# A convolution's bias moved into the residual, its relu and sum made one DVE operation, and the order of all steps written anew

## The reference

```
# 1: convolution with gates, on the group-normalised x (pairs of channels, whole image)
info = relu(info_w @ gn(x) + info_b)            # 16 channels
mask = sigmoid(mask_w @ gn(x) + mask_b)         # 16 channels
x = x + relu(out_w @ (mask outer info) + out_b) # 256 products to 64 channels
# 2: linear attention over the 1024 pixels (tokens) of an image, 8 heads, on ln(x)
K, Q = elu(ln(x) Wk) + 1, elu(ln(x) Wq) + 1
msg = ln(attention(Q, K, ln(x) Wv) Wm)
x = x + ln(x) + ln(relu([ln(x), msg] W1) W2)
# 3: mixture of 8 experts on ln(x), the two best by a softmax gate
x = x + sum over e of weight[e] * (gelu(ln(x) W1[e] + b1[e]) W2[e] + b2[e])
```

## Time and profile before

| | |
|---|---|
| median of 3 runs | 1180.87 us |
| the profiled execution, its time | 1182.04 us |
| its span, first to last instruction | 1180.2 us |
| TensorE busy | 1080.6 us (92%) |
| DVE busy | 790.7 us (67%) |
| ACT busy | 682.4 us (58%) |
| POOL busy | 363.3 us (31%) |

### The profile page before, as it was taken

One profiled execution on the slowest core, in us unless ns is written; L12 is line 12 of the kernel. 1 busy time (PEld: TensorE's weight loads), 2 busy tenths in 40 slices (PEclk: granted clock), 3 DMA queues, 4 the chain that ended last, 5 costly groups with the idle time before them and its releaser, 6 DMA issues.

```text
span 1180.2 us, 15496 instructions
## 1 busy us (share of the span) xinstructions
PE 1080.6 (92%) x5878; PEld 487.5 (41%) x5878; DVE 790.7 (67%) x1673; ACT 682.4 (58%) x930; POOL 363.3 (31%) x277
## 2 busy tenths in 40 slices
PE   3798689989999899998999999998999989999898
PEld 1463445423544246342464335442354424634232
DVE  5675836696658876587674976669665887656534
ACT  2256365665765546765656656656566555676454
POOL 0010032243313423234312433224331343324465
PEclk9999989999999999999999999999999999999999
DMA  4010097008610195003920068100861019300580
GB/s 150 1 35 3 1 216 146 19 1 199 146 36 19 30 224 126 1 19 81 225 73 1 19 144 199 36 19 0 189 156 36 19 38 226 81 1 19 120 203 21
DMA packets 17418, 96.64 MB, mean 82 GB/s; under 512 B 3648, under 2 KB 6720, under 8 KB 13120
## 3 DMA queue, kind: packets, MB, share of 16 engines
q1 hardware_dynamic: 17344, 95.66, 34.9%
HBM read 77.82 MB, written 9.44 MB: 74 GB/s over the span
## 4 chain that ended last, share of the span: by engine, by line
PE 65%; DVE 18%; ACT 12%; issue 4%; SPq 1%; DMA 0%; DVEq 0%; POOL 0%; POOLq 0%; ACTq 0%
PE HP L809 13%; PE HP L823 10%; PE R L658 6%; PE R L614 5%; PE R L745 5%; PE R L603 4%; ACT H L957 4%; PE R L594 4%; DVE SM L1141 3%; PE R L752 2%; PE R L676 2%; PE R L667 2%; DVE TM L1290 2%; PE R L823 2%; DVE SM L1057 2%
## 5 line engine op out<-in xcount | busy, mean ns | idle before, releaser
L1002 POOL TENSOR_TENSOR XB<-TM,XB 128x512 f32<-128x512 f32 x254 | 325.2, 1298 | 663.4 <-DVE TM L1290 663.4
L957 ACT ACTIVATE H<-HP,W 128x1024 f32<-128x1024 f32 x224 | 240.5, 1113 | 129.8 <-PE HP L809 129.2
L809 PE MATMUL HP<-XF,W1E 64*128 64x512 f32 x1024 | 267.9, 631 | 20.0 <-DVE TM L1290 19.6
L823 PE MATMUL HP<-H,W 128*64 128x512 f32 x896 | 232.3, 614 | 24.4 <-ACT H L957 24.4
L1290 DVE SCALAR_TENSOR_TENSOR TM<-HP,B2S,CWB 128x512 f32<-128x512 f32 x224 | 161.3, 744 | 57.1 <-PE HP L823 56.2
L1141 DVE TENSOR_REDUCE SM<-T 128x8 f32<-128x512 f32 x128 | 84.3, 681 | 109.3 <-ACT T L892 108.1
L809 PEld LDWEIGHTS HP<-XF,W1E 64*128 64x128 f32 x1024 | 84.6, 186 | 150.0 <-DVE TM L1290 84.5
L892 ACT ACTIVATE T<-R 128x512 f32<-128x512 f32 x128 | 75.2, 604 | 83.5 <-PE R L658 77.3
L823 PEld LDWEIGHTS HP<-H,W 128*64 128x64 f32 x896 | 46.7, 135 | 172.3 <-ACT H L957 135.6
L1113 DVE SCALAR_TENSOR_TENSOR BIG<-R,T 128x512 f32<-128x512 f32 x112 | 69.6, 681 | 26.8 <-PE R L594 26.6
L614 PE MATMUL R<-W,T 128*128 128x128 f32 x512 | 73.2, 283 | 7.1 <-DVE T L1160 5.6
(11 more groups left out here) (165 smaller groups left out, 1371.0 us busy)
## 6 DMA issues: line engine op xcount, KB each, us to landing
CWB<-gates_hbm SPq DMA_DIRECT2D x32, 1536.0 KB, 21.9
CWB<-gates_hbm SPq DMA_DIRECT2D x32, 512.0 KB, 10.0
BIG<-XN SPq DMA_DIRECT2D x32, 256.0 KB, 4.5
out<-XB SPq DMA_DIRECT2D x15, 512.0 KB, 3.0
X<-x SPq DMA_DIRECT2D x14, 512.0 KB, 7.2
W<-wpack SPq DMA_DIRECT2D x1, 1064.0 KB, 5.0
XF<-x SPq DMA_DIRECT2D x2, 512.0 KB, 6.2
gates_hbm<-CWR SPq DMA_DIRECT2D x16, 64.0 KB, 1.6
```

Of the source, the lines that this page charges most:

```text
L809: last = mm(HP[u % BATCH][:, half(k)], W1E[img(k), e, :], XF[img(k), 1 - par, s, half(c)], start=True, stop=True)
L823: last = mm(sums_of(b, u)[img(k), :], w("w2e")[:, C * e:C * e + C], activated(b, u)[:, k, :], start=True, stop=True)
L957: f(activated(b, u).rearrange("p k t -> p (k t)"), HP[u % BATCH][:, :], ACT.Gelu, bias=col(B1E + e))\
L1002: nc.gpsimd.tensor_tensor(acc, TM[:, u % BATCH, :], acc, ALU.add).then_inc(acc_done, 1)
```

## The change

The bias of the convolution is added to X by ACT right after the normalisation (with_bias, in the stage group_norm; two instructions of 128 x 1024 a group, in place). DVE then computes X + max(p, -b) in one operation that reads the product from PSUM; LEAST holds -b. The factor 0.5 goes into the weights ow, once, in prepare, where DVE has two more operations. The ACT function conv_out and its semaphore fall away. In the opening, TensorE waits for prep_done at the next group's group_stats and at conv_out, and no longer at info_0. SCHEDULE and OPENING are written anew.

```diff
--- before.py
+++ after.py
@@ -62,48 +62,46 @@
 
 
 SCHEDULE = [
-    ("channel_stats", "H", 1, 0), ("gates", "H", 0, 0), ("gate_tokens", "YY", 1, 2),
-    ("gate_exp", "H", 0, 0), ("group_stats", "HY", 2, 0), ("group_norm", "", 0, 2),
-    ("choose_1", "Y", 0, 0), ("info_mask_0", "HHYYH", 2, 2), ("choose_2", "", 1, 2),
-    ("info_mask_1", "HYYHH", 2, 0), ("gate_rows", "Y", 1, 0), ("info_0.0", "", 0, 1),
-    ("info_0.1", "YHH", 1, 1), ("low_0.0", "", 1, 0), ("low_0.1", "YY", 0, 2), ("high_0.0", "", 2, 0),
-    ("high_0.1", "HH", 0, 0), ("info_1.0", "YY", 0, 2), ("first_unit", "", 0, 0), ("info_1.1", "H", 1, 0),
-    ("low_1.0", "", 0, 0), ("low_1.1", "HY", 1, 0), ("high_1.0", "", 0, 0), ("high_1.1", "Y", 0, 2),
-    ("conv_out.0", "", 0, 0), ("conv_out.1", "", 0, 0), ("centre_1.0", "", 0, 0),
-    ("centre_1.1", "H", 0, 0), ("rstd_1", "", 0, 0), ("norm_1.0", "H", 2, 0), ("finish_1", "Y", 0, 1),
-    ("weights_1", "Y", 0, 1), ("features_1.0", "H", 0, 0), ("norm_1.1", "H", 1, 0),
-    ("features_1.1", "", 1, 0), ("query.0", "YY", 0, 0), ("query.1", "", 0, 0), ("key.0", "", 0, 0),
-    ("key.1", "", 0, 1), ("key_value.0", "", 0, 0), ("key_value.1", "H", 0, 1), ("kv_turn.1", "", 0, 0),
-    ("kv_turn.0", "", 1, 0), ("kv_values.1", "", 0, 0), ("kv_values.0", "H", 0, 0),
-    ("denominator", "", 1, 0), ("numerator.0", "", 0, 0), ("numerator.1", "Y", 0, 0),
-    ("attended.0", "", 0, 0), ("attended.1", "Y", 0, 2), ("message.0", "", 0, 0), ("message.1", "", 2, 0),
-    ("rstd_2", "HH", 0, 0), ("norm_2.0", "YY", 0, 0), ("norm_2.1", "", 0, 0), ("features_2.0", "", 0, 0),
-    ("features_2.1", "", 0, 0), ("finish_0", "", 0, 1), ("hidden_0.0", "HH", 0, 1),
-    ("hidden_1.0", "", 2, 0), ("hidden_out.0", "", 0, 0), ("hidden_0.1", "", 0, 0),
-    ("tokens_3.0", "", 0, 1), ("hidden_1.1", "Y", 0, 1), ("hidden_out.1", "Y", 0, 0),
-    ("tokens_3.1", "HHY", 0, 0), ("rstd_3", "YH", 0, 2), ("norm_3.1", "H", 2, 0), ("norm_3.0", "", 0, 0),
-    ("features_3.1", "", 2, 0), ("features_3.0", "YY", 0, 1), ("centre_4.0", "", 0, 1),
-    ("centre_4.1", "HHY", 0, 0), ("rstd_4", "", 0, 0), ("norm_4.0", "", 1, 0), ("norm_4.1", "Y", 1, 0),
-    ("features_4.0", "", 0, 0), ("features_4.1", "", 0, 2),
+    ("channel_stats", "H", 1, 0), ("gates", "H", 1, 0), ("gate_tokens", "YYH", 0, 0),
+    ("gate_exp", "", 2, 2), ("group_stats", "", 0, 0), ("group_norm", "HYY", 0, 2), ("choose_1", "", 0, 0),
+    ("info_mask_0", "HHYY", 0, 2), ("choose_2", "", 2, 2), ("info_mask_1", "HHYYHH", 0, 0),
+    ("gate_rows", "Y", 4, 2), ("info_0.1", "", 0, 0), ("info_0.0", "YH", 0, 0), ("low_0.1", "H", 0, 0),
+    ("low_0.0", "", 0, 2), ("high_0.1", "YYH", 2, 0), ("high_0.0", "HY", 2, 1), ("info_1.0", "", 0, 1),
+    ("info_1.1", "Y", 0, 0), ("first_unit", "H", 0, 0), ("low_1.0", "", 0, 0), ("low_1.1", "HY", 0, 0),
+    ("high_1.0", "", 0, 1), ("high_1.1", "Y", 0, 0), ("conv_out.0", "", 0, 0), ("finish_1", "", 2, 0),
+    ("conv_out.1", "", 0, 0), ("centre_1.1", "", 0, 1), ("centre_1.0", "HH", 2, 0), ("rstd_1", "", 0, 0),
+    ("norm_1.0", "Y", 0, 0), ("weights_1", "Y", 0, 1), ("features_1.0", "", 0, 0), ("norm_1.1", "H", 0, 1),
+    ("features_1.1", "H", 2, 0), ("query.0", "", 0, 0), ("query.1", "YY", 0, 2), ("key.0", "", 0, 0),
+    ("key.1", "", 0, 0), ("key_value.0", "", 0, 0), ("key_value.1", "", 0, 0), ("kv_turn.0", "H", 0, 0),
+    ("kv_turn.1", "", 0, 0), ("kv_values.0", "", 0, 0), ("kv_values.1", "", 0, 0),
+    ("denominator", "H", 2, 0), ("numerator.0", "", 0, 0), ("numerator.1", "Y", 0, 1),
+    ("attended.0", "", 0, 1), ("attended.1", "Y", 0, 0), ("message.0", "", 0, 0),
+    ("message.1", "HHYY", 2, 0), ("rstd_2", "", 0, 0), ("norm_2.0", "", 0, 0), ("features_2.0", "", 0, 2),
+    ("norm_2.1", "HH", 1, 1), ("features_2.1", "", 0, 0), ("hidden_0.0", "", 0, 1),
+    ("hidden_0.1", "", 0, 0), ("hidden_1.1", "", 1, 0), ("hidden_1.0", "", 0, 0),
+    ("hidden_out.1", "", 0, 0), ("hidden_out.0", "YY", 0, 0), ("tokens_3.1", "", 0, 0),
+    ("tokens_3.0", "H", 0, 0), ("rstd_3", "HYY", 0, 1), ("norm_3.1", "H", 0, 1),
+    ("features_3.1", "HY", 0, 0), ("norm_3.0", "", 2, 2), ("features_3.0", "Y", 2, 0),
+    ("centre_4.1", "", 0, 0), ("centre_4.0", "H", 1, 0), ("rstd_4", "HY", 0, 0), ("norm_4.1", "Y", 1, 0),
+    ("features_4.1", "", 0, 0), ("norm_4.0", "", 0, 1), ("features_4.0", "", 0, 0), ("finish_0", "", 0, 1),
 ]
 EARLY = 1
 OPENING = [
-    "channel_stats", "group_stats", "group_norm", "prepare", "info_mask_0", "info_mask_1",
-    "next channel_stats", "info_0.0", "info_0.1", "low_0.0", "high_0.0", "low_0.1", "info_1.0", "high_0.1",
-    "next group_stats", "low_1.0", "info_1.1", "low_1.1", "high_1.0", "high_1.1", "conv_out.0",
-    "conv_out.1", "centre_1.0", "centre_1.1", "rstd_1", "norm_1.0", "features_1.0", "norm_1.1",
-    "next group_norm", "features_1.1", "next info_mask_0", "next info_mask_1", "query.1", "query.0",
-    "next info_0.0", "next info_0.1", "key.1", "key.0", "next low_0.1", "key_value.1", "key_value.0",
-    "next low_0.0", "kv_turn.0", "kv_turn.1", "kv_values.0", "next high_0.1", "kv_values.1", "denominator",
-    "numerator.1", "numerator.0", "next high_0.0", "attended.1", "attended.0", "next info_1.1",
-    "next info_1.0", "message.1", "message.0", "rstd_2", "norm_2.0", "next low_1.0", "next low_1.1",
-    "features_2.0", "hidden_0.0", "norm_2.1", "features_2.1", "hidden_1.0", "hidden_0.1", "hidden_1.1",
-    "hidden_out.0", "tokens_3.0", "next high_1.0", "hidden_out.1", "tokens_3.1", "rstd_3", "norm_3.1",
-    "norm_3.0", "next conv_out.0", "features_3.1", "features_3.0", "next high_1.1", "centre_4.1",
-    "centre_4.0", "rstd_4", "norm_4.1", "norm_4.0", "next conv_out.1", "features_4.1", "features_4.0",
-    "gates", "gate_tokens", "gate_exp", "next centre_1.0", "choose_1", "choose_2", "next centre_1.1",
-    "gate_rows", "next rstd_1", "next norm_1.1", "next features_1.1", "next norm_1.0", "next features_1.0",
-    "weights_1",
+    "channel_stats", "group_stats", "group_norm", "next channel_stats", "info_mask_0", "info_mask_1",
+    "info_0.0", "low_0.0", "info_0.1", "high_0.0", "low_0.1", "info_1.0", "high_0.1", "prepare",
+    "info_1.1", "low_1.0", "low_1.1", "high_1.0", "next group_stats", "next group_norm", "conv_out.0",
+    "high_1.1", "next info_mask_0", "conv_out.1", "next info_mask_1", "centre_1.1", "centre_1.0",
+    "next info_0.0", "next info_0.1", "rstd_1", "norm_1.1", "features_1.1", "norm_1.0", "features_1.0",
+    "next low_0.1", "query.1", "next low_0.0", "query.0", "key.1", "key.0", "key_value.1", "next high_0.0",
+    "kv_turn.1", "kv_values.1", "key_value.0", "kv_turn.0", "kv_values.0", "denominator", "next high_0.1",
+    "numerator.0", "numerator.1", "attended.0", "attended.1", "message.0", "next info_1.1", "message.1",
+    "rstd_2", "next info_1.0", "norm_2.0", "next low_1.1", "norm_2.1", "next low_1.0", "features_2.0",
+    "features_2.1", "hidden_0.1", "next high_1.0", "hidden_1.1", "hidden_0.0", "hidden_1.0",
+    "next high_1.1", "hidden_out.0", "hidden_out.1", "tokens_3.1", "tokens_3.0", "rstd_3", "norm_3.0",
+    "norm_3.1", "next conv_out.0", "features_3.1", "features_3.0", "centre_4.1", "centre_4.0", "rstd_4",
+    "norm_4.0", "norm_4.1", "next conv_out.1", "features_4.0", "features_4.1", "next centre_1.1", "gates",
+    "gate_tokens", "gate_exp", "choose_1", "choose_2", "next centre_1.0", "gate_rows", "weights_1",
+    "next rstd_1", "next norm_1.1", "next norm_1.0", "next features_1.0", "next features_1.1",
 ]
 AHEAD = [name.partition(" ")[2] for name in OPENING if name.startswith("next ")]
 ROUTER = ("gates", "gate_tokens", "gate_exp", "choose_1", "choose_2", "gate_rows", "weights_1")
@@ -167,6 +165,7 @@
         W1G = sb("W1G", [P, HID])
         BH = sb("BH", [P, 1])
         BT = sb("BT", [P, 1])
+        LEAST = sb("LEAST", [P, 1])
         ONE = sb("ONE", [P, 2], BF16)
         MINUS = sb("MINUS", [P, 1])
         BI = sb("BI", [P, 2, 2])
@@ -253,7 +252,7 @@
         ir_done = sems("ir_done")
         prod_done = sems("prod_done")
         oc_ps = sems("oc_ps")
-        oc_act = sems("oc_act")
+        xb_set = sem("xb_set")
         x1_done = sems("x1_done")
         ln_ps = sems("ln_ps")
         ln_sq = sems("ln_sq")
@@ -560,6 +559,8 @@
 
                 def group_stats():
 
+                    if a == EARLY:
+                        pe.wait_ge(prep_done, 1)
                     for s in range(G):
                         pe.wait_ge(gn_stat, nth(a + 1, s))
                         mm(Ra[s][:, 0:2], w("pairavg"), ST[:, s, 12:14], start=True, stop=True).then_inc(gn_avg, 1)
@@ -577,7 +578,6 @@
                 def replicate(n, slots):
 
                     if n == 0 and starting(a):
-                        pe.wait_ge(prep_done, 1)
                         pe.wait_ge(act_prep, 2)
                     for s in slots:
                         if n == 0:
@@ -596,6 +596,8 @@
                                     last.then_inc(rep_ps[s], 1)
 
                 def conv_out(slots):
```

(34 more changed lines are left out.)

## The result

The changed kernel takes 1191.66 us (1190.32 to 1194.18, 4 runs), the kernel before, on the same chip, 1181.22 us (1180.21 to 1182.26). The ratio is 1.0089 [1.0076, 1.0103]: slower by 10.4 us, where 3.35 were forecast. The profiled execution has a span of 1190.5 us and a time of 1192.8 us.

The account below looks back on a forecast made before the run. TensorE, busy 1080.6 of 1180.2 us, was taken as the bound, leaving about 100 us idle to win. Six turns +3.9, turn 1 +0.45 and opening -1.0 gave +3.35, so 1184.2 us; range 1170 to 1192.

Parts of the forecast that it names:

- Bias on ACT: Routing stretch: bias instructions delay info_mask's ACT work and gelus, partly repaid by info_mask_1's new place; +0.4 us a turn.
- Replication: Replication stages info, low and high, paired and split anew: together 6.1 us instead of 6.7, -0.5 a turn.
- centre_1 to key: From centre_1 to key: query.1 and YY end about 0.7 before the chain to key.0; +0.3 us a turn.
- key_value: key_value.0 waits 0.4 for DVE's combines, kv_turn and kv_values then wait 0.4 less; -0.1 us a turn.
- Message to tokens_3: Normalisation hidden better (-0.15), but TensorE waits 0.4 to 0.7 for ACT's relu at hidden_1.1; +0.3 us a turn.
- Tokens_3 to features_4: H, features_3.1, H, Y, features_3.0 each wait 0.05 to 0.2 for a normalisation or combine; +0.25 us a turn.
- Sum of a turn: All terms of one full turn added: +0.65 us, bounds -0.7 to +2.2; six turns +3.9.
- Rival A: TensorE's clock also falls in the four other full turns, +3.2 us on the forecast: 1187.5 us; chance 0.14.
- B: Routing stretch: bias at 0.55 us each or less does not delay the gelus, waits are won: 1175.2 us; chance 0.20.
- C: Opening's 4.6 us head start reaches the first expert unit, engines' slack absorbs the turns' small waits: 1176 us; chance 0.13.
- D: No difference: the shifts of a turn, none over 0.5, cancel, and the opening too: 1181 us; chance 0.20.
- The opening: Before the first expert unit: it starts at 152.7 instead of 153.63, rounded to -1.0 us; bounds -5 to +3.

Follow-up runs that it names:

- experiment 4: Changed kernel with the two bias instructions issued on ACT behind info_mask_1, no longer ahead of info_mask_0: 1192.1 us, ratio 1.0101.
- experiment 9: Kernel before with only info_mask_1 moved on TensorE, to between HHYY and HHYYHH, gelus placed to fit: 1184.89 us, ratio 1.0024.
- experiment 10: Changed code with both lists of the kernel before, and only info_mask_1 moved as in experiment 9: 1184.56 us, ratio 1.0026.
- experiment 5: Changed kernel with H and Y steps put back in pairs in the replication stages and behind tokens_3: 1199.14 us, ratio 1.0159.
- experiment 6: Changed kernel with norm_1.0 ahead of norm_1.1 on DVE at the end of the opening: 1188.25 us, ratio 1.0052.
- experiment 8: Changed code, old turn list, opening rewritten: features_2 in one piece, hidden_0 before hidden_1, norm_1.0 first: 1180.21 us, ratio 0.9995 to the kernel before.
- experiment 1: Changed code with the step list and opening list of the kernel before: 1187.69 us, ratio 1.0048.
- experiment 2: Changed kernel with the opening list of the kernel before, new turn kept: 1190.44 us, ratio 1.0079.
- experiment 7: Changed kernel with the four matmuls of the next group's low_1.0 issued four times over in the opening: 1193.7 us, ratio 1.0089.
- experiment 3: Changed kernel with the turn step list of the kernel before, new opening kept: 1183.86 us, ratio 1.0026.

## Why the prediction was right, and where it was not

Direction and range held; the size was a third of the true one. There is luck in both. The measured 1191.66 lies 0.34 inside the upper end of the range, 1192, and two of its four runs lie past it. The forecast's own range (1183.3 to 1190) was passed. The bounds of the prediction itself, six times +1.58 for a turn and +4 for the opening, give 1194.5 when added as it adds them within a turn, so 1192 was narrower than its own working. And the opening, which was forecast as a gain, was a loss. By its steps, each against an undisturbed turn:

- **Bias on ACT (+0.4):** the waits came as forecast (1.25 for 1.4, 1.55 for 1.6, the 0.93 gone), but the term was +0.06. The walk followed the delay through the gelus and took the second combine for the start of choose_2. DVE ends that combine 0.24 later (8.46 for 8.22 behind the normalisation; 0.15 of it is a wait) and then wins 0.20: its operation at 543.00 takes 0.42, where the same one took 0.62 at 396.69 before, beside an addition of POOL that ended at 397.0 (rows at the end). DVE has no other idle time between the normalisation and the combine. Experiments 4, 9 and 10 show that the stretch is DVE's.
- **Replication (-0.5):** +0.21. Start to start, the replications themselves take 5.90 for 6.25, -0.35. But six H steps of the new stretch stand alone, where two pairs and two singles stood, and a Y pair is split; the expert steps take 0.55 more, which is two times 0.19 and 0.17, and I had priced them as the same. This is the first mis-sized term. That the splits are the cause is worked out here, not shown: experiment 5 brought a new wait with it.
- **conv_out (0):** right, no wait before centre_1.
- **centre_1 to key (+0.3), key_value (-0.1):** +0.16 and -0.22. The wait of 0.59 came at key.0 and the 0.4 at key_value.0 did not: the combines were through before the key steps.
- **Message to tokens_3 (+0.3):** +0.25, with 0.68 of wait at hidden_1.1 as forecast.
- **Tokens_3 to features_4 (+0.25):** +0.62. The step named waits of 0.05 to 0.2; there are none but the first (0.52, before 0.28). Up to centre_4 it is +0.75, of it 0.51 by the three splits, and experiment 5, which undoes them, gave back 0.50.
- **Turn 1 (+0.45):** +0.9.
- **Sum of a turn:** +1.08 measured, +0.65 forecast. In the five turns it shows as 0.6 each only because two falls of the clock, 1 us each, are gone from them. Rival A (falls in every turn) went the other way. B failed at its condition: the pair of bias instructions took 2.19, and even where they stood behind the first gelus (experiment 4) the stretch hardly changed. C failed in the opening (below), and D, no difference, needed a shift of nothing. After the last conv_out the list costs +0.86 up to the wait behind the last choose_2; then the fall comes that no turn had, and adds 1.5. H there takes 2.96, where the same step before took 1.99 (1100.21):

```profile
1109.02 2.96 PE L811 MATMUL HP<-XF,W1E 64*128 64x512 f32 x8 [2.89 <-DVE TM L1298]
```

- **The opening (-1.0):** this is the step that failed, +4.0. The prediction had named the sign, a first unit behind 156; it came at 157.61. Its first half was right: XF kept DVE until 15.85, info_mask_0's DVE work went at 18.60 (19.0 forecast), rstd_1's at 54.28 (55.2), and features_2 was 2.1 ahead (2 to 3 forecast). So was the 1.2 lost by norm_1.0's place (experiment 6: 4.87 to 3.67). What failed is that I carried the lead on at the upper clock, with no term for the clock in the opening, and did not walk hidden. From features_2 to features_3 it took 29.52 against 23.54 before, +6.0. Experiment 6 with the same list in this part took 27.07 under a shorter lower clock, so by this estimate some 2.4 of it are the clock. Experiment 8, another order under a still shorter one, took 24.37, so up to 2.7 more are the order (low_1.1 between the two slots of features_2 on DVE, hidden_1.1 in front of hidden_0.0) and the clock together. The two were not tried apart, and 0.8 stays over. Nor is the new list the only loss: the changed code loses 1.0 to 2.6 by the first unit with the old list too (experiments 1, 2, 10), so putting the old list back (experiment 2) won only 1.6 of the 4.0, by one profiled run each.

The trace shows when the clock fell and what TensorE did before: in the changed kernel it fell at 92.7, at the end of the wait of 1.86 before features_2, and the level came back at 106.4, in the middle of hidden. The Trainium skill ("TensorE: Matmul & The Clock Gate", section "What's actually happening") says that throttled is the default and activity releases it. The trace agrees in so far as the fall ends a wait and the level comes back in the middle of work. It doesn't tell the length: the clock stayed at 1.2 GHz over 92.70 to 106.40 although TensorE worked 12.49 of these 13.70 us. Nor did waits tell it: with the wait cut to 0.46 the fall was as long (experiment 7), and behind a wait of 3.76 it was 3.4 (experiment 8). In the turns the record is mixed. Waits of 1.25, 0.58 and 1.55 came without a fall, in the changed kernel and in experiment 10. Another 1.44 behind them (experiment 5) came with falls in four of five turns, which is for the rule. A single wait of 2.39 (experiment 9) came with falls in three turns and without in two.

**Still open:** what sets the length of the fall over hidden, and why runs of one kernel fall into groups 4 to 6 us apart (experiments 1, 3, 8). The lower clock differs from run to run: with the same opening it began with 20.5 us at the lower level in experiment 10 and not in 1, and the first unit came 1.6 apart. But the mean clock does not order the runs: in experiment 8 the runs near 1185 had 0.982 to 0.983, the profiled one of 1180.37 had 0.977. No run near 1185 of experiment 8 was profiled, so that its turns held the falls is argued, not shown.

## What to carry to other kernels

Price a matmul step by start to start, in the company that it will have: a step alone costs more than half of a pair, and here the splits cost more (0.55) than the replications gained (0.35). Find the engine whose row of work has no gap in the stretch before pricing a wait there; here moving TensorE's idle time about changed nothing. And compare turns with the same clock: here 2 of the 5.3 us lost in five turns were hidden by two falls that went elsewhere. Look at the clock once more after every change of the order: experiment 5 won its 0.50, and its profiled run is 11.9 us longer than the changed kernel's, 7.9 of them by falls in four turns.

## What the runs showed of the hardware

- ACT's 128x1024 add of a bias, SBUF to SBUF, takes 1.14 us, and a pair 2.19, so the second starts before the first ends.
- Start to start, two steps of four 64x512 float32 matmuls in one run move TensorE on by 1.92 us, a step that stands alone by 1.05 or 1.06.
- A DVE operation on two SBUF inputs, 128x256, took 0.42 us alone, 0.62 when it began 0.33 before the end of a POOL addition, and 0.93 when it began 0.64 before it (the addition of 391.63 ends at 393.08). The POOL addition behind the second took 1.46 instead of 1.27:

```profile
391.63 1.45 POOL L1002 TENSOR_TENSOR XB<-TM,XB 128x512 f32<-128x512 f32 x1
392.44 0.93 DVE L1229 TENSOR_TENSOR RT<-RT 128x256 f32<-128x256 f32 x1
...
395.75 1.27 POOL L1002 TENSOR_TENSOR XB<-TM,XB 128x512 f32<-128x512 f32 x1 [2.67 <-DVE TM L1290]
...
396.99 1.46 POOL L1002 TENSOR_TENSOR XB<-TM,XB 128x512 f32<-128x512 f32 x1
```

  The Trainium skill ("SBUF — State Buffer", section "SBUF: two separate sides") says that of two such instructions the one that starts first blocks the other until it ends. Here the trace agrees in kind: DVE lost 0.20 and 0.51, more the more of the addition was left, and the addition that began during the DVE operation lost 0.2. In the changed kernel the operation began 0.1 before the end of an addition (541.82, 1.28) and lost nothing, while the next addition (543.06) took 1.50; spans on POOL are rough, so 0.1 decides nothing.
- A fall of the clock in a turn cost 1.0 us (139.5 to 140.54), in experiment 4 0.6 to 0.7 and in experiment 5 1.6 to 2.9; one in the last part cost 1.5, and 6.9 us more of the lower clock in the opening, over hidden, about 2.4.
- The place of one stage goes with other falls: of five turns, the profiled run of experiment 10 had none with one, that of 9 three, that of the kernel before two. Each is one execution.
